# P's halves behind every fourth slot, rounded by VectorE; a shorter table load in ScalarE's last trip

## What is computed

```python
edge_index = jnp.stack([src, dst])
x_i = x[tgt]; x_j = x[src]                     # x is the layer-normalised input
feat = jnp.concatenate([x_i, x_j - x_i], axis=-1)
h = jax.nn.relu(feat @ W1 + b1)                # W1: 512 x 512
msg = h @ W2 + b2                              # W2: 512 x 256
out = jax.ops.segment_sum(msg, tgt, num_segments=num_nodes)
x = x + out / (deg + 1e-08)
x = x + ffn(layernorm(x))                      # 8 experts, top 2
```

## Time and profile before

| | |
|---|---|
| median of 3 runs | 908.91 us (908.79 to 911.26) |
| profiled execution | 910.95 us |
| its span, first to last instruction | 908.9 us |
| mean granted TensorE clock | 0.988 |
| busy in the span: PE, DVE, ACT, POOL | 853.1, 628.5, 650.0, 601.6 us |
| edge stage: first gather starts, last gather starts, last edge sum ends | 65.16, 578.45, 597.58 us |

### The profile page before, as it was taken

The page is one execution under the profiler, slowest core; times in us unless marked ns, Lnnn a source line. Parts: engine busy times, 40 slices in busy tenths (PEclk is TensorE's granted clock), DMA queues, the critical chain, the costliest instruction groups (busy, mean ns, idle before and its releaser), DMA issues. The chain is left out here.

```text
span 908.9 us, 17092 instructions
## 1 busy us (share of the span) xinstructions
PE 853.1 (94%) x4164; PEld 670.7 (74%) x4165; DVE 628.5 (69%) x1716; ACT 650.0 (72%) x1444; POOL 601.6 (66%) x615
## 2 busy tenths in 40 slices
PE   9988998999999998998999999989999999999997
PEld 5446776776667676766777767668888999999996
DVE  6947887787878787777887777646884455554553
ACT  4427888898899898989999999735555555555553
POOL 2227777777777777777777777349404577776864
PEclk9998999999999999999999999979999999999999
DMA  8557877788778787887887878619852444443443
GB/s 252 170 162 226 256 242 235 238 248 246 237 236 249 236 246 232 250 241 238 242 244 235 237 240 258 155 32 271 271 155 47 64 67 78 72 77 65 79 69 49
DMA packets 90977, 169.26 MB, mean 186 GB/s; under 512 B 17608, under 2 KB 56910, under 8 KB 90840
## 3 DMA queue, kind: packets, MB, share of 16 engines
q0 software_dynamic: 43696, 122.35, 49.4%
q1 hardware_dynamic: 46232, 44.79, 16.9%
q10 hardware_dynamic: 944, 0.92, 0.3%
HBM read 146.98 MB, written 21.43 MB: 185 GB/s over the span
## 5 line engine op out<-in xcount | busy, mean ns | idle before, releaser
L984 POOL DMA_INDIRECT gath<-q_rows,idx_t x408 | 390.2, 956 | 137.3 <-issue 88.1
L1039 DVE SCALAR_TENSOR_TENSOR h_lo<-bank,h_hi 128x512 fp32r<-128x512 f32 x327 | 222.8, 686 | 85.7 <-ACT h_hi L1206 82.9
L1190 ACT ACTIVATE bank<-gath 128x512 f32<-128x512 f32 x327 | 198.3, 607 | 22.4 <-DMA gath<-q_rows,idx_t 19.9
L1206 ACT ACTIVATE h_hi<-bank 128x512 fp32r<-128x512 f32 x327 | 193.6, 597 | 25.3 <-PE agg_ps L1405 8.9
L1346 PE MATMUL bank<-p_hi,ohT 128*128 x327 | 138.4, 423 | 32.1 <-ACT bank L1190 21.4
L1404 PE MATMUL agg_ps<-h_hi,oh 128*128 128x512 f32 x408 | 162.7, 399 | 5.0 <-DVE h_lo L1039 5.0
L1405 PE MATMUL agg_ps<-h_lo,oh 128*128 128x512 f32 x408 | 162.0, 397 | 0.0
L1347 PE MATMUL bank<-p_lo,ohT 128*128 x327 | 129.3, 396 | 0.0
L1346 PEld LDWEIGHTS bank<-p_hi,ohT 128*128 128x128 f32 x327 | 61.8, 189 | 80.9 <-issue 69.6
L1967 POOL DMA_INDIRECT out<-y_out,sca_i x56 | 92.7, 1655 | 41.1 <-issue 15.7
L2071 PE MATMUL bank<-tokT,fw_now 128*128 128x128 f32 x896 | 109.3, 275 | 0.8 <-ACT tokT L2027 0.8
(11 more groups left out here) (286 smaller groups left out, 1242.8 us busy)
## 6 DMA issues: line engine op xcount, KB each, us to landing
rows_sb<-rel_blocks SPq DMA_DIRECT2D x102, 128.0 KB, 4.4
fw<-in_L_ffn_W SPq DMA_DIRECT2D x16, 512.0 KB, 5.1
gath<-q_rows,idx_t POOLq DMA_INDIRECT x408, 4.4
q_rows<-q_buf SPq DMA_DIRECT2D x25, 256.0 KB, 2.7
out<-x_all SPq DMA_DIRECT2D x28, 128.0 KB, 4.1
x_all<-in_x SPq DMA_DIRECT2D x25, 128.0 KB, 2.5
xm_rows<-xt SPq DMA_DIRECT2D x25, 128.0 KB, 3.6
x_all<-in_x SPq DMA_DIRECT2D x2, 640.0 KB, 10.1
```

Of the source, the lines that this page charges most:

```text
L984: pool.indirect_dma_start(out=gath[:, j % RING, :], out_offset=None, in_=q_rows[:, :], in_offset=bass.IndirectOffsetOnAxis(ap=idx_t[:, j:j ...
L1039: dve.scalar_tensor_tensor(out=h_lo[:, j % LO_RING, :], in0=z_of(slot0, j), scalar=0.0, in1=h_hi[:, j % HI_RING, :].bitcast(F32), op0=ALU. ...
L1190: actv.activation(z_of(slot0, j), gath[:, j % RING, :], ACT.Copy).then_inc(s_seed, 1)
L1206: actv.activation(h_hi[:, j % HI_RING, :], z_of(slot0, j), ACT.Relu).then_inc(s_hi, 1)
```

## The change

- Halves stand behind every fourth slot from slot 7: half m of P behind slot 4m + 7, the last behind slot 187. Five groups of four slots follow without one; the two halves of W2 stand behind slots 211 and 215, the gain products behind 219. SP's load of W2 and of x's last tile moves from its group 94 to group 48 (`W2_AT`).
- P's halves are rounded by DVE (`tensor_copy` into `p_hi`, with a wait for its own end ahead of the subtraction) in place of ACT. The semaphore `s_hi` counts only what ACT still makes (`hi_at`, `hi_no`).
- `build_oh` stands behind `split_lo` of its slot, and in the first pass the two waits for `s_sum` that other waits imply are left out.
- ACT's last trip loads 3 + 1 tile numbers in place of 17.
- `first_ok`, the table by which the kernel finds out whether a tile's P is made in time, follows the new places.

```diff
-HALF_PERIOD = 8
+NODE_TILES = 25
+HALF_PERIOD = 4
+W2_GAP = 5
 def half_after(j):
-    return j // HALF_PERIOD if j % HALF_PERIOD == HALF_PERIOD - 1 else None
+    if j % HALF_PERIOD != HALF_PERIOD - 1:
+        return None
+    m, halves = j // HALF_PERIOD - 1, PARTS * (NODE_TILES - READY)
+    return None if m < 0 else m if m < halves else m - W2_GAP if m >= halves + W2_GAP else None
...
+        rounded = [what for what in steps if what[0] == "slot" or what[1] >= P_HALVES]
+        hi_at = {what: k for k, what in enumerate(rounded)}
...
-                W2_AT = HALF_PERIOD * P_HALVES // GROUP + 2
+                W2_AT = HALF_PERIOD * (P_HALVES + 1) // GROUP + 1
...
                 def split_lo(slot0, j):
-                    wait_after(dve, s_hi, step_no(slot0, j))
-                    wait_after(dve, s_sum, slot0 + j - LO_RING)
+                    wait_after(dve, s_hi, hi_no(slot0, j))
+                    if not isinstance(slot0, int):
+                        wait_after(dve, s_sum, slot0 + j - LO_RING)
...
                 def low_half(m):
-                    wait_after(dve, s_hi, step_at["half", m])
+                    if m < P_HALVES:
+                        dve.wait_ge(s_half_ps, m + 1)
+                        dve.tensor_copy(half_of(p_hi, m), half_bank(m)).then_inc(s_high, 1)
+                    else:
+                        wait_after(dve, s_hi, hi_at["half", m])
...
+                    dve.wait_ge(s_high, m + 1)
                     dve.tensor_tensor(half_of(p_lo, m), half_bank(m), half_of(p_hi, m).bitcast(F32), ALU.subtract).then_inc(s_lo, 1)
...
+                        split_lo(0, j)
                         if j % GROUP == 3 and j // GROUP + 3 < NG:
-                            build_oh(0, j // GROUP + 3)
-                        split_lo(0, j)
+                            build_oh(0, j // GROUP + 3, freed_by_hi=True)
...
                 def high_half(m):
+                    if m < P_HALVES:
+                        return
...
-                    actv.activation(half_of(p_hi, m), half_bank(m), ACT.Copy).then_inc(s_hi, 1)
...
+                        left = min(UNROLL, NS - slot0)
+                        ends = range(0, left + 1, GROUP)
+                        vals = dict(zip(ends, load_tiles(mybir.EngineType.Activation, local0, len(ends), GROUP)))
                         if slot0 + UNROLL >= NS:
-                            return load_tiles(mybir.EngineType.Activation, local0, UNROLL + 1)
-                        ends = range(0, UNROLL + 1, GROUP)
-                        return dict(zip(ends, load_tiles(mybir.EngineType.Activation, local0, len(ends), GROUP)))
+                            vals[left - 1], = load_tiles(mybir.EngineType.Activation, local0 + left - 1, 1)
+                        return vals
```

More of the change, by code:

```diff
@@ L92, in build @@
     BATCH = 5
-    assert NT % 2 == 1 and 2 * H == 1024 and D == 256 and f_w1.shape[2] == H and f_w2.shape[2] == D
+    assert NT == NODE_TILES and NT % 2 == 1 and 2 * H == 1024 and D == 256 and f_w1.shape[2] == H and f_w2.shape[2] == D
     def row(v):
@@ L443, in _ @@
                                    pattern=[[1, P]], channel_multiplier=-1).then_inc(s_const, 1)
-                pool.iota(first_ok[:, :], pattern=[[PARTS * HALF_PERIOD, 32]], base=FIRST_RING - (READY - 1) * PARTS * HALF_PERIOD, channel_multiplier=0,
+                pool.iota(first_ok[:, :], pattern=[[PARTS * HALF_PERIOD, 32]], base=FIRST_RING + HALF_PERIOD - (READY - 1) * PARTS * HALF_PERIOD, channel_multiplier=0,
                           allow_small_or_imprecise_dtypes=True).then_inc(s_const, 1)
@@ L827, in build @@
         s_half_ps = sem("s_half_ps")
+        s_high = sem("s_high")
         s_xback = sem("s_xback")
@@ L846, in step_no, with hi_no @@
             return step_at["slot", slot0 + j] if isinstance(slot0, int) else slot0 + (j + HALVES)
+        rounded = [what for what in steps if what[0] == "slot" or what[1] >= P_HALVES]
+        hi_at = {what: k for k, what in enumerate(rounded)}
+        def hi_no(slot0, j):
+            return hi_at["slot", slot0 + j] if isinstance(slot0, int) else slot0 + (j + HALVES - P_HALVES)
         def z_of(slot0, j):
@@ L1019, in _, with build_oh @@
                 here = [None]
-                def build_oh(slot0, q):
-                    wait_after(dve, s_sum, slot0 + (q - 3) * GROUP - 1)
+                def build_oh(slot0, q, freed_by_hi=False):
+                    if not freed_by_hi:
+                        wait_after(dve, s_sum, slot0 + (q - 3) * GROUP - 1)
                     local = here[0] + q * GROUP
@@ L1192, in high_half @@
                 def high_half(m):
+                    if m < P_HALVES:
+                        return
                     actv.wait_ge(s_half_ps, m + 1)
                     if m == HALVES - 1:
-                        wait_after(actv, s_hi, step_at["half", m] - 1)
+                        wait_after(actv, s_hi, hi_at["half", m] - 1)
                         actv.sem_inc(s_hi, 1)
@@ L1199, in high_half @@
                         actv.activation(w2_turned[m - P_HALVES], z_bank[step_at["half", m] % FIRST_RING], ACT.Copy).then_inc(s_hi, 1)
-                        return
-                    actv.activation(half_of(p_hi, m), half_bank(m), ACT.Copy).then_inc(s_hi, 1)
                 def relu_hi(slot0, j):
@@ L1359, in half_product @@
                     if m == HALVES - 1:
-                        wait_after(pe, s_hi, step_at["half", m - 1])
+                        wait_after(pe, s_hi, hi_at["half", m - 1])
                         for h in range(KH):
```

## The result

The changed kernel took 901.45 us in the median of four runs (900.72 to 904.58), the kernel before 908.91 (908.79 to 911.26). The ratio is 0.9911, 95% interval [0.9891, 0.993]: 7.5 us faster. The profiled execution took 904.58 us with a span of 902.8; it is the slowest of the four.

What follows compares the result with a forecast made beforehand. POOL's gathers set the pace, so savings show only in the tail: load 2.6 + arrears 2.4 + clock 3.2 = 8.2 us, the middle costing nothing; 908.91 - 8.2 = 900.7, say 900.8 us, range 898 to 906.

Steps and rivals of the forecast that it cites:

- a serial tail behind the last gather: From the last gather to the next stage's first matmul, 22.1 us: 8.2 us saved if POOL stays as fast.
- (a): ACT's last trip in the tail: loading 3 + 1 numbers instead of 17 saves 2.6 us, bounds 2.0 and 2.8.
- (b): Compute engines' lateness at slot 407: seed ends 7.0 us after its gather's start, not 9.4; saves 2.4 us (0 to 3.8).
- (c): PE's clock in the tail: stays full after a shorter standstill, speeding sums, count products and next stage; 3.2 us (0 to 3.8).
- rival 1: Tail: PE's clock falls all the same after a 2.4 to 3.0 us standstill; 5.0 us saved, 903.9; chance 0.28.
- PE in the middle: Edge stage up to slot 187: PE's group with a half takes 4.91 us against POOL's 5.04; price 0.
- rival 2: Middle: PE's groups take 5.4 us if the register load isn't hidden; slower, 911 to 914; chance 0.09 together with another rival.
- DVE: Edge stage: DVE takes over the rounding at 0.5 us, its group then 4.6 us of 5.04.
- W2 and the rows behind it: Around slots 183 to 190: DVE may wait 1 to 5 us for rows, PE behind it; nothing on POOL.
- The ring: Edge stage: 16 gathers let 11 more slots, 13.9 us of arrears, pile up before POOL waits.
- POOL: Gathers in the edge stage: builds start at other moments, so slow gathers change by 0 in sum, bounds -2 and +4.
- rival 3: Gathers: the build falls at the bad phase in each of 102 groups; slower, 917; chance 0.09 together with another rival.

Runs made afterwards that it cites:

- load alone: Kernel before with only ScalarE's last-trip register load shortened; halves, rounding and build_oh as before: 905.13 us, ratio 0.9951.
- long load: Changed kernel with the old load of 17 numbers back in ScalarE's last trip: 906.01 us, ratio 0.9961.
- ScalarE rounding: Changed kernel with the rounding of P's halves put back on ScalarE, at the new places: 902.63 us, ratio 0.9932.
- the four with a loaded middle: Changed kernel with one (ratio 0.9964) or three (1.0015, again 1.0011) further zero products per P half, or W2's load two groups later (0.9943).
- new places alone: Kernel before with halves, W2 and first_ok as in the changed kernel; ScalarE rounds and loads as before: 907.1 us, ratio 0.9974.
- W2 later: Changed kernel with SP's load of W2 two groups later, group 50 in place of 48: 1043.26 us, ratio 0.9943.

## Why the prediction was right, step by step

It said 900.8 us (898 to 906); it is 901.45. The path (a serial tail behind the last gather, a middle that costs nothing) is borne out by the runs. The terms:

- **(a) The load, 2.6 us.** Measured 2.60 and 2.61 us in the two pairs that differ in it alone by its code (before and load alone; long load and changed kernel). The working by numbers per load held to a tenth of a us.
- **(b) The arrears, 2.4 us (0 to 3.8).** The last seed was to end 7.0 us after its gather's start; it ended 7.04 after it. With the new places the five traces give 6.4 to 7.9, with the old ones 9.4 and 10.9. The mean gain, 10.2 less 7.0, is 3.2 us; a single execution moves by over 1 us. Part of that goes with the clock some 20 us ahead of the tail, which the sum didn't have. Over 566 to 578 us PE's mean granted clock was 1.00 in three of the traces with the new places, 0.86 in the changed kernel, with ScalarE rounding and in the kernel before, and 0.72 with the load alone. From slot 393's seed to slot 400's the arrears moved by -0.2 to 0.1 us in the first three, rose by 1.5 and 1.1 in the next two, by 2.5 in the kernel before and by 3.7 with the load alone. The last two have the gain products there: at the same clock of 0.86 they go with 1.0 to 1.4 us more, where the prediction put about 3.
- **(c) The clock, 3.2 us (0 to 3.8).** The size came out between what the two cases give, and the reason was wrong for the trace at hand. Where the clock holds, the trace gives 1.26 us up to the last sum, 1.20 to the next stage and 1.22 up to its third tile, 3.7 in all, where 1.3, 1.3 and 0.6 were put. In the changed kernel's trace it fell, which was rival 1. But rival 1 gave the fall no gain at all, as if the clock stayed down for 10.2 us as before; it was down for 3.4, and 2.3 of the 3.7 us came all the same (0.22 + 0.83 + 1.22). The argument "a standstill of 3.0 is nearer to 2.3 than to 4.97" was the weak one: of seven standstills at this place from 2.21 to 2.37 us, five kept the clock (the trace with ScalarE rounding, and the four with a loaded middle) and two lost it (2.21 in the changed kernel, 2.36 with the load alone). A length alone doesn't decide. The same is seen 20 us earlier: ahead of slot 392's expand PE stands still for 2.05 to 2.45 us in all five traces with the new places, and the clock falls behind it in two (after 2.05 and 2.31 us) and not in three (2.27, 2.32, 2.45).
- **PE in the middle.** A half's group was to take 4.91 us. In the changed kernel one half starts at 166.14 and the next group's at 171.07, 4.93 us later, with POOL's group at 5.06:

```profile
166.14 1.05 PE L1402 MATMUL deg_ps<-w_wide,x_all 128*128 128x264 f32 x4
...
171.07 1.03 PE L1402 MATMUL deg_ps<-w_wide,x_all 128*128 128x256 f32 x4
```

So rival 2 didn't come about: no wait of POOL over 0.3 us, and at slots 104 to 184 a seed was 5.6 to 6.1 us behind its gather (5.6 to 7.2 before).

- **DVE.** The rounding was put at 0.5 us. It takes 0.42, and the subtraction behind it starts 0.47 after it:

```profile
168.01 1.01 DVE L1040 TENSOR_SCALAR oh<-iota_row,rel_t 128x128 fp32r<-128x128 f32 x4
168.79 0.42 DVE L1076 CAST p_hi<-deg_ps 128x256 fp32r<-128x256 f32 x1
169.26 0.42 DVE L1098 TENSOR_TENSOR p_lo<-deg_ps,p_hi 128x256 fp32r<-128x256 f32 x1
```

- **W2 and the rows behind it.** DVE was to wait 1 to 5 us at slot 190. It waited 5.71 us, once. PE waited 2.56 us as well, but not behind DVE, since it went on at 316.04, 1.9 us before DVE did:

```profile
307.83 0.38 SPq L987 DMA_DIRECT2D w_wide<-in_L_gnn_W  x1
310.24 8.57 SPq L374 DMA_DIRECT2D rows_sb<-rel_blocks  x3
...
316.04 0.49 PE L1368 MATMUL bank<-p_hi,ohT 128*128 x1 [2.56 <-ACT bank L1210]
317.98 0.49 DVE L1047 TENSOR_SCALAR ohT<-rows_sb,slot_no 128x512 fp32r<-128x512 bf16 x1 [5.71 <-DMA rows_sb<-rel_blocks]
```

PE waited for a seed, and that seed for the rows of its gather (timeline of ACT; then the landing of the gathers of 309:317, of all gathers, and of `rows_sb` in 305:322):

```profile
315.30 0.60 ACT L1210 ACTIVATE bank<-gath 128x512 f32<-128x512 f32 x1 [2.75 <-DMA gath<-q_rows,idx_t]
...
DMA to landing us min/median/max: 4.9/6.8/7.5
...
DMA to landing us min/median/max: 3.4/4.3/7.5
...
DMA to landing us min/median/max: 4.5/9.2/9.4
```

So while W2, tiles of x and three sets of rows were under way together, gathers took up to 7.5 us to land in place of 4.3, and the rows 9.2. That is the term that was mis-sized: the prediction took the rows at 4.3 to 8.4 us and the gathers as untouched. The seed of slot 200 was 10.3 us behind its gather, 4 more than before, and that of slot 248 was back at 6.4. The ring took it up, as the prediction had it (3 to 8 us of arrears in all); the wait just passed the upper end given.

- **POOL, 0 (-2 to +4).** Its stage took 1.37 us more in the changed kernel: 44 of 408 gathers took over 0.97 us (35 before), and only 6 of the 46 new casts touch a slow one. But the load alone, which moves no half, has 44 slow ones too and 514.57 us, while the four other traces with the new places take 512.9 to 513.3. So by these traces the 1.4 us belong to the execution, not to the change. The Trainium skill (SBUF — State Buffer, Who interferes with whom) has a VectorE instruction with at most one SBUF input, outside the 2-port modes, not contend with GpSimd; the casts, which read PSUM, bear that out.

The prediction's reading of the slow gathers was wrong, though. It put them down to a `build_oh` that begins 0.7 to 0.9 us after the gather's start. With the old places 17 of the 23 gathers in which one began after 0.65 to 0.95 us were slow; in the changed kernel, where `build_oh` has moved, none of 22 was. What the traces with either placing share is the other build, `build_ohT`. In the changed kernel it ended 0.15 to 0.42 or 0.85 to 1.0 us after the start of 33 gathers, and 32 of these are slow; of the 49 after whose start it ended at another moment within 1 us, none is. Over the seven traces of the table it is 183 of 189 and 1 of 329. A slow gather then ends 0.82 us after the build, or 0.12 us after it in the late case (timelines of POOL and DVE, changed kernel; the build ends at 136.58, the gather at 137.41):

```profile
136.24 1.17 POOL L997 DMA_INDIRECT gath<-q_rows,idx_t  x1 [0.30 <-ACT bank L1210]
...
136.09 0.49 DVE L1047 TENSOR_SCALAR ohT<-rows_sb,slot_no 128x512 fp32r<-128x512 bf16 x1 [0.36 <-PE bank L1369]
```

The slow gather of the earlier trace rows fits as well (DVE, kernel before): a `build_ohT` ended at 178.09, 0.37 us after its start and 0.82 before its end, and the `build_oh` of rows 9 merely came next.

```profile
177.60 0.49 DVE L1033 TENSOR_SCALAR ohT<-rows_sb,slot_no 128x512 fp32r<-128x512 bf16 x1 [0.54 <-PE deg_ps L1347]
```

The 12 slow gathers without a `build_ohT` lie over a `build_oh`, and of the 4.9 us that the gathers of the changed kernel take over 0.948 each, 3.9 are with a `build_ohT`. So rival 3 looked at the wrong build; that POOL cost nothing was right, but not for its reason.

In the pair of profiles, then, the load and the arrears came as put (2.6 and 2.4 us), the clock gave 1.05 us up to the next stage and 0.78 behind it, where 3.2 were put in all, POOL cost 1.37, and 0.65 were gained at the front by chance. In the other traces with the new places POOL's cost is gone, and (b) is larger in the mean over all traces. Two of the prediction's own signs came out against it in the changed kernel's trace: the clock behind the standstill was not 1.00, and 44 gathers were over 0.97 us where 35 was the limit. So the total was met because such differences offset each other, not because each term was exact.

## What to carry to other kernels

When one engine sets the pace of a long stage, read the stretch between its last instruction and the next stage's first: it is serial, and what is saved in it adds up one for one. Work that the other engines have late in the stage is best moved early, where the ring's slack takes it up (even after a wait of 5.7 us no gather was held, and the arrears were gone 50 slots later), and a register load, which costs 0.21 us a number, should hold only what the loop still uses and come before the pace-setter has ended.

## What the runs showed of the hardware that was not expected

- TensorE's clock after a standstill: lost in two of seven of 2.21 to 2.37 us, 2.0 and 2.3 us after PE's last product had ended, and given back 3.4 us later. In the three of 4.84 to 4.98 us it was always lost, but only 4.0 to 4.3 us after the stop, and for different times: 3.4 us with the long load, 10.2 with the new places alone and in the kernel before. What decides on either is open.
- Where VectorE's `build_ohT` slowed a gather, it did so almost only at two moments: the build ended 0.15 to 0.42 or 0.85 to 1.0 us after the gather's start (183 of 189 such gathers were slow, 1 of 329 others). It cost up to 0.26 us each time, 2.9 to 4.4 us in the 408 gathers of a trace.
- The same program has an edge stage of 513 us or, at other times, one of 643 to 649 us, in which engines stand still without a releaser in the profile, while gathers, seeds, relus and `h_lo` take as long as ever (962, 603, 597 and 686 ns with W2 later; 960, 603, 595 and 685 in the changed kernel). PE's mean clock is lower there, 0.93 to 0.96 in place of 0.98 to 0.99; which is the cause of which is open. The chips' numbers were the same in both, so they don't tell the two apart. A comparison is worth something only beside the kernel before, run then and there, and an experiment on slack says nothing where the bound has moved to another engine.
